# A Mamba, expert and attention block on one core: the second half's input work inside the first scan, the first half's routing inside the second scan

## What is computed

```
x = x + mamba_moe(ln(x))     # changed here
x = x + ffn(ln(x));  x = x + attention(ln(x));  x = x + ffn(ln(x))

mamba_moe(h0):
  h   = rmsnorm(h0) ; xi, z = split(h @ in_proj)          # 256 channels each
  xi  = silu(causal_conv4(xi) + conv_b)                   # per channel
  dt, B, C = split(xi @ x_proj)                           # 64, 16, 16
  delta = softplus(dt @ dt_proj + dt_b)
  for n in 16 states:  s_n[t] = exp(delta[t] * A_n) * s_n[t-1] + delta[t] * xi[t] * B_n[t]
  y   = sum_n s_n * C_n + D * xi ;  r = h0 + (y * silu(z)) @ out_proj
  g   = rmsnorm(r) ; probabilities = softmax(g @ router) ; the best 2 of 8 experts
  return r + sum over the 2 of  p_e * (silu(g @ Wg_e) * (g @ Wu_e)) @ Wd_e
```

## Time and profile before

| | |
|---|---|
| median of 3 runs | 722.12 us |
| the profiled execution | 728.63 us, its span 726.9 us |
| PE busy | 570.0 us (78% of the span) |
| DVE busy | 488.5 us (67%) |
| ACT busy | 384.8 us (53%) |
| POOL busy | 331.7 us (46%) |
| first scan | 49.8 to 145.9 us |
| second scan | 191.8 to 296.4 us |
| expert stage begins | about 306 us |

### The profile page before, as it was taken

How to read it: one execution, slowest core, us unless ns; L and a number is a source line. 1 busy time by engine, 2 the same in 40 slices (tenths; PEclk the granted TensorE clock), 3 DMA queues, 4 the chain that set the end, 5 groups by cost and what they waited for, 6 DMA issues and landing times.

```text
span 726.9 us, 11045 instructions
## 1 busy us (share of the span) xinstructions
PE 570.0 (78%) x3447; PEld 361.2 (50%) x3447; DVE 488.5 (67%) x1310; ACT 384.8 (53%) x604; POOL 331.7 (46%) x289
## 2 busy tenths in 40 slices
PE   1938667788467576798779999975779989989887
PEld 1413223244122232497779989952545545545456
DVE  5549999954798899635323475358877787886053
ACT  1586555525654455266346756732446666566731
POOL 5259989800799999132666532531111112111010
PEclk9978999899587998999889999995999999999999
DMA  5736456401387855120114200323203103000001
GB/s 142 278 114 191 156 168 177 127 0 35 128 256 208 243 178 170 32 69 16 42 46 115 86 19 15 100 76 84 54 9 84 30 2 96 12 2 2 2 14 46
DMA packets 50523, 65.91 MB, mean 91 GB/s; under 512 B 7730, under 2 KB 29250, under 8 KB 50210
## 3 DMA queue, kind: packets, MB, share of 16 engines
q1 hardware_dynamic: 45122, 59.27, 27.8%
q0 software_dynamic: 2496, 5.15, 1.9%
q10 hardware_dynamic: 2848, 0.78, 0.5%
HBM read 47.46 MB, written 9.52 MB: 78 GB/s over the span
## 4 chain that ended last, share of the span: by engine, by line
PE 40%; DVE 8%; issue 5%; ACT 4%; ACTq 1%; another core or an unknown queue 0%; POOL 0%; DMA 0%; POOLq 0%; DVEq 0%
PE ps L1507 37%; DVE arena L1427 3%; ACT arena L1056 2%; PE ps L1766 1%; DVE x L1362 1%; DVE nb L1155 1%; DVE stats L1142 1%; PE ps L1656 1%; PE ps L1773 1%; ACTq L1046 0%; ACT arena L1076 0%; ACT arena L1064 0%; ACT r L1056 0%; DVE mv L1145 0%
## 5 line engine op out<-in xcount | busy, mean ns | idle before, releaser
L1507 PE MATMUL ps<-arena 128*128 128x128 f32 (+11 forms) x2150 | 328.3, 330 | 45.2 <-DVE arena L1427 17.5
L1507 PEld LDWEIGHTS ps<-arena 128*128 128x128 f32 (+2 forms) x2150 | 211.7, 160 | 129.0 <-issue 57.2
L1507 PE MATMUL ps<-arena,ident 128*128 128x512 f32 x256 | 137.8, 685 | 69.4 <-DVE arena L1298 69.4
L1288 DVE TENSOR_TENSOR_SCAN arena<-ps,arena 128x512 f32<-128x512 f32 x128 | 147.8, 1202 | 9.2 <-POOL arena L821 6.3
L1427 DVE CUSTOM_DVE_ANT_0 arena<-ps,cmask 128x128 f32<-128x128 f32 (+3 forms) x256 | 111.5, 487 | 26.5 <-PE ps L1507 26.2
L821 POOL TENSOR_TENSOR arena<-arena 128x1024 f32<-128x1024 f32 x64 | 128.6, 2029 | 0.6
L997 ACT ACTIVATE ps<-arena 128x512 f32<-128x512 f32 x128 | 88.0, 690 | 76.2 <-DVE arena L1288 73.4
L1507 PEld LDWEIGHTS ps<-arena,ident 128*128 128x128 f32 x256 | 52.9, 219 | 150.8 <-DVE arena L1298 97.7
L1481 DVE TENSOR_TENSOR arena<-arena,ps 128x512 f32<-128x512 f32 x46 | 31.7, 688 | 78.0 <-PE ps L1507 41.0
L806 POOL DMA_INDIRECT moe_out<-arena,xT x46 | 45.5, 989 | 82.3 <-DVE arena L1451 71.6
L1056 ACT ACTIVATE arena<-ps 128x1024 f32<-128x1024 f32 (+3 forms) x86 | 57.0, 709 | 36.3 <-PE ps L1507 35.9
(11 more groups left out here) (191 smaller groups left out, 604.3 us busy)
## 6 DMA issues: line engine op xcount, KB each, us to landing
arena<-bc_rows SPq DMA_DIRECT2D x128, 256.0 KB
arena<-arena SPq DMA_DIRECT2D x64, 64.0 KB
arena<-arena SPq DMA_DIRECT2D x28, 128.0 KB, 2.5
moe_rows<-arena SPq DMA_DIRECT2D x2, 1495.0 KB, 11.8
arena<-moe_rows SPq DMA_DIRECT2D x8, 325.0 KB, 4.7
arena<-in_L_attn_a_Wg SPq DMA_DIRECT2D x8, 256.0 KB
arena<-in_L_attn_a_Wu SPq DMA_DIRECT2D x8, 256.0 KB
arena<-moe_out SPq DMA_DIRECT2D x4, 512.0 KB, 4.5
```

Source lines behind the costliest of these rows:

```text
L1288: V.tensor_tensor_scan(hst[:, g % STATES, e, :], bank(6 + e), dBx[:, g % RING, e, :], 0.0, ALU.mult, ALU.add).then_inc(s_scan, 1)
L1507: return T.matmul(o, l, rr, start=start, stop=stop)
```

## The change

While the first scan runs, PE also makes the second half's in projection and the convolution of its channel half 0, in bank 5, one matmul or two taps at a time (`AHEAD`), and ACT copies each result out (`COPY_AT`): xi to `xip`, the convolution to `xc`, and z without SiLU to a new buffer `zr`, which lies over weights no longer needed. After the scan DVE makes the second half's convolutions at once, ahead of the gate; ACT makes all SiLUs; x_proj, dt_proj and softplus follow tile by tile; the first half's out projection comes behind them on PE, and its residual and moments between the two deltas on DVE.

The routing of the first half moves into the second scan at fixed states (`ROUTE_AT`: norm 35, turn 36, copies 38, router 39, logits 41, top_a 42, exp 43, top_b 44, rank 45, slots 47). The scatters move from the states 34 to 49 to the states 48 to 63. SP stores the rows of the two tiles apart. Some small buffers of the routing move to PSUM, the router and rank banks change, and the two weight semaphores become one. `ON_POOL` is as before.

```diff
+        z_at = at[0] - 11 * P - 2 * 3 * HID
+        zr = arena[:, z_at:z_at + CT * HL].rearrange("p (e l) -> p e l", e=CT)
...
-        ridf = carve([2, TH])
-        req = carve([2, TH, NE])
+        ridf = ps[:, 4, 64:64 + 2 * TH].rearrange("p (k t) -> p k t", k=2)
+        req = (ps[:, 4, 128:128 + TH * NE].rearrange("p (t e) -> p t e", t=TH), carve([TH, NE]))
...
+        AHEAD = {1: ("xi", 0, 0), 3: ("xi", 0, 1), 5: ("xi", 1, 0), 7: ("xi", 1, 1), 9: ("taps", 0, 0), 10: ("taps", 0, 1),
+                 13: ("z", 0, 0), 15: ("z", 0, 1), 17: ("taps", 1, 0), 18: ("taps", 1, 1), 21: ("z", 1, 0), 23: ("z", 1, 1)}
+        COPY_AT = {3: ("xi", 0, 0), 5: ("xi", 0, 1), 7: ("xi", 1, 0), 9: ("xi", 1, 1), 12: ("taps", 0, 1),
+                   15: ("z", 0, 0), 17: ("z", 0, 1), 20: ("taps", 1, 1), 23: ("z", 1, 0), 25: ("z", 1, 1)}
+        first_1 = NS * HB
+        ROUTE_AT = {"h2norm": first_1 + 3, "h2turn": first_1 + 4, "input": first_1 + 6, "router": first_1 + 7,
+                    "logits": first_1 + 9, "top_a": first_1 + 10, "exp": first_1 + 11, "top_b": first_1 + 12,
+                    "rank": first_1 + 13, "slots": first_1 + 15}
...
+            def store_rows(b):
+                sp.wait_ge(s_dts, b + 1)
+                sp.dma_start(bc_rows[b], dts[RK:RK + 2 * NS, b % HB, :]).then_inc(s_bt, 16)
             for h in range(HB):
-                for b in range(HB * h, HB * h + HB):
-                    sp.wait_ge(s_dts, b + 1)
-                    sp.dma_start(bc_rows[b], dts[RK:RK + 2 * NS, b % HB, :]).then_inc(s_bt, 16)
                 first, end = state_of(HB * h, 0), state_of(HB * h + HB, 0)
-                sp.wait_ge(s_bt, 16 * HB * (h + 1))
                 for g in range(first, end):
+                    if g == first:
+                        store_rows(HB * h)
+                        sp.wait_ge(s_bt, 16 * (HB * h + 1))
+                    elif g == first + BS:
+                        store_rows(HB * h + 1)
+                    elif g == first + NS:
+                        sp.wait_ge(s_bt, 16 * (HB * h + 2))
                     spread_b(g)
...
+                        if h and c == 0 and n == 2:
+                            powers(0, 2 * TB)
+                        j = c * NS + n - NS
                         if h and 0 <= j < 2 * TH:
                             scatter(0, j // 2, j % 2)
-                powers(2 * TB * h, 2 * TB)
+            powers(2 * TB, 2 * TB)
...
+            def relu_abs(h, c):
+                for e in range(CT):
+                    act.wait_ge(s_dtp, 2 * (HB * h + c) + e + 1)
+                    S.activation(v[:, c, e, :], bank((2, 6)[c] + e), ACT.Relu, bias=dtb[:, e:e + 1])
+                    last = S.activation(u[:, c, e, :], bank((2, 6)[c] + e), ACT.Abs, bias=dtb[:, e:e + 1])
+                ch.link(last)
+            def exp_log(c):
+                ch.link(S.activation(u[:, c, :, :], u[:, c, :, :], ACT.Exp, scale=-1.0))
+                S.activation(u[:, c, :, :], u[:, c, :, :], ACT.Ln, bias=1.0).then_inc(s_u, 1)
...
+            def inputs_1():
+                act.wait_ge(s_cvc, HB)
+                act.wait_ge(s_zc, 2 * HB)
+                for c in range(HB):
+                    cs = slice(c * L, c * L + L)
+                    S.activation(xc[:, 0, cs], xc[:, 0, cs], ACT.Silu, bias=convb[:, 0:1]).then_inc(s_xc, 1)
+                for e in range(CT):
+                    for c in range(HB):
+                        cs = slice(c * L, c * L + L)
+                        S.activation(zr[:, e, cs], zr[:, e, cs], ACT.Silu).then_inc(s_zs, 1)
+                for c in range(HB):
+                    act.wait_ge(s_cd, HB + c + 1)
+                    S.activation(xc[:, 1, c * L:c * L + L], v[:, c, 1, :], ACT.Silu, bias=convb[:, 1:2]).then_inc(s_xc, 1)
+                    if c == 0:
+                        row_copy(1, 0)
+                S.preload_act_table_set("natural_log_exp_and_others")
+                relu_abs(1, 0)
+                row_copy(1, 1)
+                exp_log(0)
+                relu_abs(1, 1)
+                exp_log(1)
+            def copy_ahead(what, c, e):
+                cs = slice(c * L, c * L + L)
+                if what == "xi":
+                    act.wait_ge(s_ip, 8 + 2 * c + e + 1)
+                    S.copy(xip[:, c, e, 4:4 + L], bank(5)).then_inc(s_xi, 1)
+                elif what == "z":
+                    act.wait_ge(s_ip, 12 + 2 * c + e + 1)
+                    S.copy(zr[:, e, cs], bank(5)).then_inc(s_zc, 1)
+                else:
+                    act.wait_ge(s_cv, HB + c + 1)
+                    act.wait_ge(s_dx, c + 1)
+                    S.copy(xc[:, 0, cs], bank(5)).then_inc(s_cvc, 1)
+            for h in range(HB):
+                (inputs_0, inputs_1)[h]()
...
+                        if g in COPY_AT:
+                            copy_ahead(*COPY_AT[g])
+                        if g == ROUTE_AT["input"]:
+                            moe_input(0)
+                            moe_input(1)
+                        if g == ROUTE_AT["logits"]:
+                            logits(0)
+                        if g == ROUTE_AT["exp"]:
+                            router_exp(0)
...
+            def form_delta(b):
+                c = b % HB
+                dve.wait_ge(s_u, b + 1)
+                V.tensor_tensor(delta[:, :, c * L:c * L + L], v[:, c, :, :], u[:, c, :, :], ALU.add).then_inc(s_dl, 1)
+            def add_residual(h):
                 for c in range(HB):
                     b = HB * h + c
...
+                    dve.wait_ge(s_op, b + 1)
+                    V.tensor_tensor(r[:, tiles(b), :], bank((0, 6)[h] + c).rearrange("p (j d) -> p j d", j=TB),
+                                    r[:, tiles(b), :], ALU.add).then_inc(s_r, 1)
+                dve.wait_ge(s_r, HB * h + HB)
+                sl = tiles_of(h)
+                moments(r, HB * h, 2 * TB)
+                ch.link(V.tensor_tensor(small[:, 3, sl], mv[:, sl, 0], mv[:, sl, 0], ALU.mult))
+                ch.link(V.tensor_tensor(small[:, 3, sl], small[:, 3, sl], mv[:, sl, 1], ALU.add))
+                count["var"] += 1
+                V.tensor_scalar(small[:, 1, sl], small[:, 3, sl], EPS, None, ALU.add).then_inc(s_var, 1)
...
+                if h == 0:
+                    for b in range(HB):
+                        conv_1(b)
+                    for b in range(HB):
+                        form_delta(b)
+                else:
+                    form_delta(HB)
+                    add_residual(0)
+                    form_delta(HB + 1)
...
+                        if g == ROUTE_AT["h2norm"]:
+                            h2_norm(0, count["var"])
+                        if g == ROUTE_AT["top_a"]:
+                            top_a(0)
+                        if g == ROUTE_AT["top_b"]:
+                            top_b(0)
+                        if g == ROUTE_AT["slots"]:
+                            find_slots(0, rank_bank(0))
                 weigh(state_of(HB * h + HB, -1))
+                if h == 0:
+                    conv_1(HB)
+                    conv_1(HB + 1)
                 gate(HB - 1)
...
+            add_residual(1)
...
+            def out_proj(h):
+                pe.wait_ge(s_yg, 2 * h + 2)
+                for c in range(HB):
+                    for j in range(TB):
+                        for e in range(CT):
+                            last = mm(ps[:, (0, 6)[h] + c, j * P:j * P + P], zs[:, e, c * L + j * P:c * L + j * P + P],
+                                      opw[:, e, :], start=(e == 0), stop=(e == CT - 1))
+                    last.then_inc(s_op, 1)
...
+            def inputs_1():
+                pe.wait_ge(s_wpc, NPREP)
+                pe.wait_ge(s_xc, 2 * HB + 3)
+                x_proj(1, 0)
+                dt_proj(1, 0)
+                pe.wait_ge(s_xc, 2 * HB + 4)
+                pe.wait_ge(s_zc, 2 * HB)
+                x_proj(1, 1)
+                dt_proj(1, 1)
+                out_proj(0)
+            def ahead(what, c, e):
+                if what == "xi":
+                    wait(pe, s_xi, 2 * HB + 2 * c + e if c or e else 0)
+                    mm(bank(5), ipw[:, e * P:e * P + P], mamba_in(1, c)).then_inc(s_ip, 1)
+                elif what == "z":
+                    if e:
+                        pe.wait_ge(s_zc, 2 * c + 1)
+                    else:
+                        pe.wait_ge(s_cvc, c + 1)
+                    mm(bank(5), ipw[:, (2 + e) * P:(3 + e) * P], mamba_in(1, c)).then_inc(s_ip, 1)
+                elif e == 0:
+                    pe.wait_ge(s_xi, 4 * HB)
+                    wait(pe, s_zc, 2 * c)
+                    taps(bank(5), c, (0, 1))
+                else:
+                    taps(bank(5), c, (2, 3)).then_inc(s_cv, 1)
+            for h in range(HB):
+                (inputs_0, inputs_1)[h]()
...
+                    if g in AHEAD:
+                        ahead(*AHEAD[g])
+                    if g == ROUTE_AT["h2turn"]:
+                        turn_h2(0)
```

(41 more changed lines are left out.)

173 lines of the change are left out of this document (57 added, 116 removed).

## The result

The changed kernel takes 725.45 us, the median of 5 runs (723.78 to 727.42), against 722.12 of the kernel before (5 runs by then, 720.75 to 722.17). That is 3.3 us more by the medians; the ratio, 1.0058 [1.0043, 1.0074], stands for 4.2. The profiled executions stand the other way round (722.9 us of span after, 726.9 before): in that one execution of before, the same code behind the scans took 426.1 us from the last gate's start to the end, for 417.9 in after, and in the 100 us from 311 on the granted clock was 0.90 for 0.97. So the scans are compared, and what lies behind them by itself.

What follows compares the result with a forecast made beforehand. DVE was taken to set the pace late in the second scan, a chain of short stages the gap; -21.6 + 1.8 + 1.7 + 17.9 + 1.4 = +1.2 us on 722.12 gave 723.3, range 719.0 to 728.0.

Steps and rivals of the forecast that it cites:

- A: The forecast itself, all five parts summed: 723.3 us, own range 721.0 to 726.0, chance 0.52.
- Part 1: Gap between the scans: shrinks from 45.9 to 24.3 us, a gain of 21.6.
- E+18.3: Start of DVE's second residual add in the gap, 18.3 us after E, the end of state 31's last scan.
- Part 2: First scan: ACT's added copies delay decays at seven of ten places, +1.8 us; bounds 0 and 5.7.
- Part 3: States 32 to 45: POOL waits go, norm and routing work come in, +1.7 us to 51.4; bounds 49.4 and 54.
- rival D: First scan: ACT's copies stand in the decay chain, up to 5.7 us; shared interface would add; 727.2, chance 0.24.
- Part 4: States 46 to 63: six weighings and all scatters meet in POOL's queue, +17.9 us to 72.8; bounds 57.6 and 76.
- Part 5: End of second scan: PE's sums before the gate run slower after an idle 5 us, +1.4 us; bounds 0 and 1.7.
- B: Second tile: POOL's queue does not bind, scatters mostly waiting; part 4 +2.7, part 5 zero; 706.7, chance 0.08.
- C: A's mechanism, but first-scan copies absorbed, norm and h2T copies too, no overlap in delta; 719.4, chance 0.13.
- E: Gap: only half the gain comes, since stages put side by side are in series; 10.8 more, 734.1, chance 0.03.

Runs made afterwards that it cites:

- e3: Changed kernel with ACT's ten copies in the first scan, and PE's pieces with them, moved to states where the decay has slack; ratio to before 1.0087.
- e5: Changed kernel with copies moved as in e3 and the first two z projections one state later, at 16 and 18; ratio to before 1.0079.
- e6: Changed kernel with six POOL weighings in states 32 to 47, three in the last tile, routing two to three states earlier, copies as in e5; ratio to before 0.9972.
- e9: e8 with the first scan's copies placed as in e5; ratio to before 0.9888.
- e2: Changed kernel with the 8 scatters for the second expert issued by POOL after the second scan; ratio to before 0.9947.
- after_again: The changed kernel run once more, unaltered, on chip 0; ratio to before 1.0090.
- e1_again: Second run of e1, on a chip where the kernel before is quicker; ratio to before 0.9943.
- e1: Changed kernel with ON_POOL of tiles 2 and 3 exchanged, so POOL weighs six states in tile 2, two in tile 3; ratio to before 0.9917.
- e4: Changed kernel with DVE's residual adds and moments put ahead of both deltas in the gap; ratio to before 1.0119.
- e7: Changed kernel with inputs still made ahead, but first-half routing in series in the gap and scatters back at states 34 to 49; ratio to before 1.0001.
- e8: Changed kernel with POOL weighing 5, 7, 9, 11, 13 in tile 2, 5, 10 in tile 3, last four scatters behind the scan; ratio to before 0.9891.
- before_again: The kernel before run once more, unaltered, for a second profile; ratio to before 1.0008.

## Why the prediction was right

Forecast +1.2 us, measured +3.3 by the medians and +4.2 by the ratio; 723.3 against 725.45, inside 719 to 728 and inside A's own range. Two parts of this are luck. Misses of +2.0 and +1.1 us are half hidden by one of -1.4; and in the second series, on chip 0, the ratio of the same two kernels, 1.0090, would be 728.6 on before's 722.12, just beyond the range. The likeliest number also stood for a change too small to be told, and the kernel is slower clear of noise, as the chances had it with 0.44. What holds is the mechanism, the gain in the gap and the loss at POOL's queue. Step by step, with after's profiled execution:

**Part 1 (24.3, measured 26.34).** The chain is as forecast: x_proj, the delta after ACT's first Ln, residual, moments, last delta. The second add starts 0.9 later than E+18.3, through hand-overs. The overlap with POOL was rightly seen and put on the wrong instruction: the last delta took 1.22 (2.39 was forecast), as POOL's three dBx had just ended; the moments before it paid 2.45 instead. That the price was one big operation's doubling is thus wrong. In before, the delta at 187.44 came 1.04 us behind the start of POOL's dx, which ended at 188.75, and was done 1.08 us after that end, which is about its own time. POOL of before:

```profile
186.40 2.35 POOL L811 TENSOR_TENSOR arena<-arena 128x1024 f32<-128x1024 f32 x1 [25.60 <-DVE arena L1277]
```

So it had waited for the dx to end, and the price falls on whatever DVE operation contends with POOL, large or small, and starts under one of POOL's.

**Part 2 (+1.8, measured +2.0).** The waits before scans 6 (0.21), 8 (0.15), 10 (0.81), 13 (0.14), 21, 24 (0.14 each) and 26 (0.55) are put down to ACT's decays: the seven places that the forecast names. The waits for POOL before scans 14 and 16 (0.69 and 0.46 in before) have shrunk to nothing and 0.15, as forecast. The first tile's gate waits 0.60 for PE, which the forecast had at nothing. The scan stays under the 100 us that would have refuted the term. That the waits are the copies' is shown by e3, e5, e6 and e9: with the copies moved, those before scans 8, 13, 21 and 24 are gone, and those before 10 and 26 are back at about the 0.32 and 0.06 of before; where PE had its upper level at the gate, the scan took 96.27 and 97.11 us.

The wait before scan 6 has a second cause that the forecast left out. It is 0 in e2, 0.21 in after, 0.81 in after_again and 1.45 in e1_again, with the same order in the first scan. In state 5 ACT's copy of the C row, which stands ahead of the decay, waits for that row's DMA: 0.27, 0.44, 1.04 and 1.68 us. ACT of e1_again:

```profile
65.83 0.59 ACT L1049 COPY ps<-arena 128x512 f32<-128x512 f32 x1 [1.68 <-DMA arena<-bc_rows]
```

Before has such a wait too (0.46), and no xi copy behind it: there DVE doesn't wait. This one place is most of the spread of the first scan, 97.89 to 99.54 us.

**Part 3 (+1.7, measured +2.8).** The wrongly sized term is the norm beside POOL, +0.4 forecast and +1.7 measured; the one wait that is left ahead of a decay, 0.81 at scan 39, was forecast at 1.0:

```profile
187.57 3.37 DVE L1363 TENSOR_SCALAR nb<-r,small 128x128 f32<-128x128 f32 x8
...
214.42 1.02 DVE L1270 TENSOR_TENSOR wtok<-wtok,m 128x64 f32<-128x64 f32 x1
```

It is 3.37 us for 1.66 with POOL idle, and top_a's subtraction has 1.02 for 0.22 in before. In e1, where POOL works without a pause from 183.09 to 191.31, the norm takes more still. DVE of e1_again:

```profile
186.16 6.21 DVE L1363 TENSOR_SCALAR nb<-r,small 128x128 f32<-128x128 f32 x8
```

and its POOL:

```profile
183.09 3.95 POOL L841 TENSOR_TENSOR arena<-arena 128x1024 f32<-128x1024 f32 x2
187.00 2.35 POOL L853 TENSOR_TENSOR arena<-arena 128x1024 f32<-128x1024 f32 x1
189.31 2.00 POOL L841 TENSOR_TENSOR arena<-arena 128x1024 f32<-128x1024 f32 x1
```

The norm is eight equal operations. Taken one by one, five of them take 0.27 us each in e1_again and the first three 0.97, 2.38 and 2.03. The second and the third:

```profile
187.05 2.38 DVE L1363 TENSOR_SCALAR nb<-r,small 128x128 f32<-128x128 f32 x1
189.35 2.03 DVE L1363 TENSOR_SCALAR nb<-r,small 128x128 f32<-128x128 f32 x1
```

They end at 189.43 and 191.39, each 0.08 us after the end of the POOL operation that had started just before it (189.35 and 191.31). In after, POOL has one dBx under the norm, and it is the third of the eight that waits for its end. DVE and POOL of after:

```profile
187.95 2.02 DVE L1363 TENSOR_SCALAR nb<-r,small 128x128 f32<-128x128 f32 x1
187.79 2.09 POOL L841 TENSOR_TENSOR arena<-arena 128x1024 f32<-128x1024 f32 x1 [1.36 <-DVE arena L1386]
```

So the price is neither a doubling nor a factor of four: each time that such an operation of DVE starts under one of POOL's, it ends when POOL's does. That is one POOL operation in after and three in e1.

The Trainium skill's GPSIMD Engine Reference (Key points: GpSimd and VectorE share SBUF interfaces, and DVE contends with two SBUF inputs or in a two-port mode) was weighed and given a place only in rival D. The trace agrees that they contend, and on the two SBUF inputs: delta, the two small multiplications and top_a's subtraction (all with both inputs in SBUF) waited, while the residual add, with one input in PSUM, took 0.69 us beside POOL as with it idle, and the eight moment operations, with one input, 1.65 us beside it (1.64 in e4 with it idle). The norm has one tensor and per-partition scalars as inputs; by which of the two conditions it contends, no run shows.

**Part 4 (+17.9, measured +18.05).** 72.96 us against 72.8. The units of 3.2 and 5.5 us per state, the wait for the slots (the first scatter starts 9.73 us behind state 46, 9.65 forecast) and the fixed order of POOL's queue hold; e2 and e7 show that it is the scatters there.

**Part 5 (+1.4, measured 0).** PE does start after a pause, of 3.31 us instead of 5. In after:

```profile
299.59 5.43 PE L1593 MATMUL ps<-arena,ident 128*128 128x512 f32 x12 [3.31 <-DVE arena L1396]
```

and in after_again:

```profile
299.49 8.28 PE L1593 MATMUL ps<-arena,ident 128*128 128x512 f32 x12 [3.31 <-DVE arena L1396]
```

and the gate follows (DVE of after_again; in after it starts at 305.06 after 3.08 of idle, as in the earlier trace rows):

```profile
307.81 1.23 DVE L1403 TENSOR_TENSOR arena<-ps,arena 128x1024 f32<-128x1024 f32 x1 [5.93 <-PE ps L1593]
```

The granted clock is 1.00 over the twelve records of the first and 0.65 over those of the second. One execution has nothing of it and the other 2.85 us, over the bound of 1.7: the term exists in some executions only. Of the five profiles whose end has this order (after, after_again, e3, e4, e5), four have it, with 1.7 to 3.1 us, so that after's own was the lucky one.

**What was not in the sum.** The first scan starts 1.02 us later in after, mostly since the first in-projection matmuls ran slower (16 records in 9.50 us, 8.66 before). e8 starts at 49.63 and e6 at 49.45, before's 49.8 or earlier, so this is no part of the change. The terms' misses are +2.0, +0.2, +1.1, +0.1 and -1.4; with +1.0 for the start they make the 3.1 between +1.2 and the 4.3 of the two traces.

Of the rivals, B is refuted. C had the last delta right (1.22 us), but the moments ahead of it paid instead, and its other two terms went the other way. D's copies didn't show in full though its shared interface did, and E's series did not come.

## What to carry to other kernels

Before work is moved under a loop, write down what every engine's queue issues per step of it, with its place in the order: two loads that are each affordable (six weighings and sixteen scatters on POOL) cost 14.5 us of waiting when they meet in the same states, and about half came back by moving either. Price a DVE operation that contends with POOL (both inputs in SBUF, and the norm here) by what POOL does at that moment, not by the row of its quiet twin: here even the smallest could cost as much as one POOL operation, some 2 us. And split a change of two halves: the half that was neutral and the half that lost are told apart by one kernel.

## What the runs showed of the hardware

- An indirect DMA of 128 rows holds POOL's queue: 1.01 us busy and 0.2 around it between two dBx, 1.26 per scatter by e2. Issued back to back at the end of e8 they start 1.27 us apart.
- Two operations of 128x8 on DVE took 0.17 us each with POOL idle and 0.87 and 1.92 beside its 128x1024 tensor_tensor. It goes both ways: POOL's dx took 3.25 us instead of 2.36 beside DVE's delta. In every such pair that was read here (delta and dx of before and of e4, the small multiplications, top_a's subtraction, the norm in after and e1_again) the operation that started later was held until the earlier one ended, and the earlier one was not slowed.
- The granted clock behind the scans differs between executions of identical code. Busy time, 311 to 411 us, of before:

```profile
311.00:411.00 100.00, 88.15 (x700) 85.65 (x700) 35.65 (x114) 55.81 (x86) 50.99 (x51) 0.90 0.19 54
```

and of before_again:

```profile
311.00:411.00 100.00, 92.57 (x792) 90.85 (x792) 44.14 (x143) 64.14 (x99) 56.32 (x56) 0.97 0.21 64
```

From the last gate to the end these took 426.1 and 417.0 us. What sets which of the two an execution gets is open. Part of it goes with the chip: the four profiles of chip 14 (e1_swap to e4) took 428.5 to 431.2 us there at 0.90 or 0.91, the eight of chip 0 took 415.7 to 419.0. But the profiled execution of before, with 426.1, took 728.63 us where the median of its runs is 722.12, so the chip isn't all of it.
